# Retention stage: outputs of both chunks of a pair together, scores of both chunks together at the end of TensorE's step, their masks in the next step

## What is computed

```python
# X (1, 2048, 128); L, D, F, H = 4, 128, 256, 8; DH = 16
def _retention(x, Wq, Wk, Wv, Wg, Wo, gn_s, gn_b, Dm, cos, sin):
    Q = (x @ Wq).reshape(B, S, H, DH)
    K = (x @ Wk).reshape(B, S, H, DH)
    V = (x @ Wv).reshape(B, S, H, DH)
    Q = _rotate(Q, cos, sin)
    K = _rotate(K, cos, -sin)
    att = jnp.einsum('bnhd,bmhd->bhnm', Q, K) * Dm     # Dm: causal decay per head
    Y = jnp.einsum('bhnm,bmhd->bnhd', att, V)
    ...                                                 # Y normalised per head, * gn_s + gn_b
    G = jax.nn.swish(x @ Wg)
    return G * Y @ Wo
for i in range(L):
    Yr = _retention(_layer_norm(X, ln_scale, ln_bias), Wq[i], ...) + X
    X = jax.nn.gelu(_layer_norm(Yr, ln_scale, ln_bias) @ W1[i]) @ W2[i] + Yr
```

## Time and profile before

| what | value |
|---|---|
| time, median of 3 runs | 599.06 us (598.79 to 599.08) |
| the profiled execution, its own time | 599.84 us |
| its span in the profile | 598.0 us |
| PE busy | 539.7 us, 90% of the span |
| DVE busy | 492.8 us, 82% |
| ACT busy | 359.2 us, 60% |
| POOL busy | 210.1 us, 35% |
| granted PE clock, mean | 0.984 |

### The profile page before, as it was taken

How to read it: one execution, slowest core, us unless ns; L and a number is a source line. 1 busy time by engine, 2 the same in 40 slices (tenths; PEclk the granted TensorE clock), 3 DMA queues, 4 the chain that set the end, 5 groups by cost and what they waited for, 6 DMA issues and landing times. The chain is left out here.

```text
span 598.0 us, 14018 instructions
## 1 busy us (share of the span) xinstructions
PE 539.7 (90%) x4372; PEld 413.8 (69%) x4372; DVE 492.8 (82%) x1825; ACT 359.2 (60%) x830; POOL 210.1 (35%) x223
## 2 busy tenths in 40 slices
PE   0899999999999999999988897898299999897994
PEld 0666787878878788787866465896155777466992
DVE  6799888988888888888899797788958999993663
ACT  2677887777877778777767675686234220132760
POOL 2354353442533425335250055375200000072671
PEclk9999999999999999999999999899699999998999
DMA  8949999993000000000000311222100000012315
GB/s 304 372 141 189 180 184 179 186 188 58 3 1 2 2 2 3 2 1 2 2 2 2 103 43 55 80 78 76 32 0 1 2 0 2 1 50 58 101 54 158
DMA packets 61130, 43.29 MB, mean 72 GB/s; under 512 B 4641, under 2 KB 58273, under 8 KB 60801
## 3 DMA queue, kind: packets, MB, share of 16 engines
q1 hardware_dynamic: 56160, 35.42, 28.7%
q0 software_dynamic: 2496, 5.13, 2.6%
q10 hardware_dynamic: 2400, 1.84, 1.0%
HBM read 18.38 MB, written 24.01 MB: 71 GB/s over the span
## 5 line engine op out<-in xcount | busy, mean ns | idle before, releaser
L471 POOL TENSOR_TENSOR att<-att,small 128x512 f32<-128x512 f32 x63 | 80.7, 1282 | 170.7 <-ACT att L360 170.7
L368 ACT ACTIVATE xz<-resid,nmr,rs 128x128 f32<-128x128 f32 x128 | 56.7, 503 | 8.6 <-DVE nmr L838 8.6
L1042 POOL DMA_INDIRECT rows_back<-ffn_yt,ffn_front x46 | 47.0, 1021 | 41.5 <-DVE ffn_yt L1393 40.3
L360 ACT ACTIVATE att<-banks 128x512 f32<-128x512 f32 x63 | 38.3, 607 | 38.3 <-PE banks L518 38.3
L1222 PE MATMUL banks<-ffn_xtT,ffn_wt 128*128 128x128 f32 x368 | 51.7, 286 | 2.2 <-DVE ffn_hr L1387 2.2
L709 DVE TENSOR_TENSOR att<-banks,small 128x512 f32<-128x512 f32 x64 | 44.0, 688 | 9.3 <-PE banks L518 9.1
L1222 PEld LDWEIGHTS banks<-ffn_xtT,ffn_wt 128*128 128x128 f32 x368 | 47.4, 202 | 3.1 <-ACT ffn_wt L1069 2.4
L518 PE MATMUL banks<-qexp,qkT 32*128 32x256 f32 x512 | 45.7, 426 | 1.7 <-DVE att L709 1.2
L489 POOL TENSOR_TENSOR qk<-cosq,sinq 128x512 f32<-128x512 f32 x32 | 40.9, 1277 | 13.9 <-DVE cosq L765 13.5
L894 PE MATMUL banks<-small 128*128 128x512 f32 (+1 forms) x74 | 31.4, 543 | 13.6 <-POOL osc_taps L1465 11.5
L1033 POOL DMA_INDIRECT rows_in<-ffn_front,ffn_slot x32 | 31.9, 998 | 29.0 <-DVE ffn_slot L1305 20.5
(11 more groups left out here) (259 smaller groups left out, 1443.8 us busy)
## 6 DMA issues: line engine op xcount, KB each, us to landing
rows_in<-zero_rows SPq DMA_DIRECT2D x16, 1032.0 KB, 18.3
shared_tab<-in_rot SPq DMA_DIRECT2D x3, 1024.0 KB, 12.6
routed_sb<-in_routed SPq DMA_DIRECT2D x1, 3072.0 KB, 12.3
ffn_front<-rows_in SPq DMA_DIRECT2D x46, 64.5 KB, 1.9
ffn_yg<-rows_back SPq DMA_DIRECT2D x8, 256.0 KB, 3.7
shared_tab<-in_rot ACTq DMA_DIRECT2D x1, 1024.0 KB, 10.3
w<-in_W SPq DMA_DIRECT2D x2, 512.0 KB, 7.3
times<-in_times SPq DMA_DIRECT2D x1, 1024.0 KB, 4.9
```

Source lines behind the costliest of these rows:

```text
L360: act.activation(att[:, c, HALF:HEADS].rearrange("p (r e) n -> p r e n", e=PER_TILE), b_att[:, 2:4, c], ACT.Copy).then_inc(s["att_raw"], 1)
L368: ins = act.activation(xz[:, n], resid[:, (g % GROUPS) * 2 + n % 2], ACT.Identity, scale=rs[:, n:n + 1], bias=nmr[:, n:n + 1])
L471: pool.tensor_tensor(att[:, c, HALF:HEADS], att[:, c, HALF:HEADS], spread(causal.unsqueeze(1), 1, HALF), ALU.mult) \
L1042: pool.indirect_dma_start(rows_back, bass.IndirectOffsetOnAxis(ap=token, axis=0), yt[:, j % RING], None).then_inc(stored[j % RING], 16)
```

## The change

The scores of both chunks of group t-1 stand together at the end of PE's step t, as eight matmuls behind one wait, and raise `att_ready` once. Their copies and masks, for both chunks, stand in the next step on ACT, POOL and DVE. Both chunks' outputs stand together: first the two matmuls with the state (each raises the new semaphore `state_read`, for which the next state waits in place of `y_ready`), then the sixteen with the masked scores. The turn of the outputs and its copy (`outputs_turned` on PE, `outputs_kept` on ACT) move into the step after. All four programs are cut into named functions, and put in a new order, with an order of their own for the last steps.

ACT and POOL:

```diff
                 def raw_scores(g, c):
 
                     wait(act, s["y_ready"], 2 * g + c - 1)
-                    wait(act, s["att_ready"], 2 * g + c + 1)
+                    wait(act, s["att_ready"], g + 1)
                     act.activation(att[:, c, HALF:HEADS].rearrange("p (r e) n -> p r e n", e=PER_TILE),
                                    b_att[:, 2:4, c], ACT.Copy).then_inc(s["att_raw"], 1)
...
-                    if coming(t):
-                        for n in range(2):
-                            c = 2 * (t + AHEAD_IN) + n
-                            ins = act.activation(resid[:, c], xin[:, c], ACT.Identity, scale=rs[:, 4 + n:5 + n],
-                                                 bias=nmr[:, 4 + n:5 + n])
...
                     lo, hi = (0 if on(0) else 2), (4 if on(6) else 2)
                     if hi > lo:
                         wait(act, s["xzt_ready"], t + 1)
                         act.activation(xzT[:, lo:hi].rearrange("p a b -> p (a b)"),
                                        b_xv[:, lo * P:hi * P], ACT.Identity,
                                        scale=lnsb[:, 0:1], bias=lnsb[:, 1:2]).then_inc(s["xzT_sb"], 1)
-                    if on(1):
...
-                        wait(act, s["gyt_ready"], g - 3)
-                        wait(act, s["ytok_ready"], g + 1)
-                        act.activation(yc[:, v].rearrange("p a b -> p (a b)"), b_y[:, 0:256], ACT.Copy) \
-                           .then_inc(s["yc_sb"], 1)
+                        g, v = t - 1, (u - 1) % RING
+                        wait(act, s["qkT_sb"], g + 1)
+                        wait(act, s["att_ready"], g - 1)
+                        for e in range(PER_TILE):
+                            ins = act.activation(qexp[:, v % 2, :, e, :], qkT[:, v, 0], ACT.Copy,
+                                                 scale=headmask[:, e:e + 1])
+                        ins.then_inc(s["qexp_act"], 1)
+
+                def step(t, u, on):
+                    if t < STEPS + 2:
+                        tables_doubled(t, u, on)
+                        mlp_rows(t, u, on)
+                        rows(t, u, on)
+                        input_rows(t, u, on)
+                        values_copied(t, u, on)
+                        first_raw(t, u, on)
+                        outputs_kept(t, u, on)
+                        second_raw(t, u, on)
+                        heads_scaled(t, u, on)
+                        squares(t, u, on)
+                        qk_copied(t, u, on)
+                        rows_copied(t, u, on)
+                        outputs_copied(t, u, on)
+                        mlp_hidden(t, u, on)
+                        queries_by_head(t, u, on)
...
-                def step(t, u, on):
+                def constants(t, u, on):
...
+                def rotated(t, u, on):
                     if on(1):
                         g, v = t - 1, (u - 1) % RING
                         wait(pool, s["rot_ready"], g + 1)
...
+                def first_masked(t, u, on):
+                    if on(2):
+                        masked(t - 2, 0)
+
+                def second_masked(t, u, on):
                     if on(2) and t != STEPS + 1:
                         masked(t - 2, 1)
-                    if on(1):
-                        masked(t - 1, 0)
+
+                def step(t, u, on):
+                    constants(t, u, on)
+                    rotated(t, u, on)
+                    first_masked(t, u, on)
+                    second_masked(t, u, on)
```

PE:

```diff
-                def scores(g, v, c):
-
+                def scores(g, v):
                     wait(pe, s["qexp_act"], g + 1)
-                    wait(pe, s["att_raw"], 2 * g + c)
-                    wait(pe, s["att_masked"], 2 * g + c)
-                    for r in range(4):
-                        rows = slice(32 * r, 32 * r + 32)
-                        ins = pe.matmul(b_att[:, r, c], qkT[rows, v, 1, c],
-                                        qexp[rows, v % 2, c], start=True, stop=True)
+                    wait(pe, s["att_raw"], 2 * g)
+                    wait(pe, s["att_masked"], 2 * g)
+                    for c in range(2):
+                        for r in range(4):
+                            rows = slice(32 * r, 32 * r + 32)
+                            ins = pe.matmul(b_att[:, r, c], qkT[rows, v, 1, c],
+                                            qexp[rows, v % 2, c], start=True, stop=True)
                     ins.then_inc(s["att_ready"], 1)
 
-                def outputs(g, v, c):
-
-                    wait(pe, s["state_ready"], 2 * g + c)
-                    if c == 0:
-                        wait(pe, s["yc_sb"], g)
-                    wait(pe, s["att_masked_rest"], 2 * g + c + 1)
-                    wait(pe, s["att_masked"], 2 * g + c + 1)
-                    out = b_y[:, c * P:c * P + P]
-                    pe.matmul(out, state[:, c], qkT[:, v, 0, c], start=True, stop=False,
-                              skip_group_check=True)
-                    for e in range(2):
-                        for q in range(4):
-                            ins = pe.matmul(out[32 * q:32 * q + 32, :],
-                                            ve[:, v, c, q, e].rearrange("p j d -> p (j d)"),
-                                            att[:, c, 2 * q + e, :], start=False, stop=(e == 1),
-                                            skip_group_check=True)
-                    ins.then_inc(s["y_ready"], 1)
+                def outputs(g, v):
+                    wait(pe, s["yc_sb"], g)
+                    wait(pe, s["state_ready"], 2 * g + 1)
+                    for c in range(2):
+                        pe.matmul(b_y[:, c * P:c * P + P], state[:, c], qkT[:, v, 0, c], start=(c == 0), stop=False,
+                                  skip_group_check=True).then_inc(s["state_read"], 1)
+                    for c in range(2):
+                        wait(pe, s["att_masked_rest"], 2 * g + c + 1)
+                        wait(pe, s["att_masked"], 2 * g + c + 1)
+                        for e in range(2):
+                            for q in range(4):
+                                ins = pe.matmul(b_y[32 * q:32 * q + 32, c * P:c * P + P],
+                                                ve[:, v, c, q, e].rearrange("p j d -> p (j d)"),
+                                                att[:, c, 2 * q + e, :], start=False, stop=(e == 1),
+                                                skip_group_check=True)
+                        ins.then_inc(s["y_ready"], 1)
...
+                def outputs_turned(t, u, on):
+                    if on(3):
+                        wait(pe, s["yT_sb"], t - 2)
+                        for c in range(2):
+                            ins = pe.transpose(b_y[:, c * P:c * P + P], yT[:, c], eye)
+                        ins.then_inc(s["ytok_ready"], 1)
...
+                def both_scores(t, u, on):
+                    if on(1):
+                        scores(t - 1, (u - 1) % RING)
+
+                def step(t, u, on):
+                    if t == 4:
+                        pe.wait_ge(s["loaded_w"], 16 * N_W)
+                    if t < STEPS + 2:
+                        outputs_turned(t, u, on)
+                        project(t, u, on)
+                        mlp_down(t, u, on)
+                        heads_turned(t, u, on)
+                        rows_turned(t, u, on)
+                        qk_turned(t, u, on)
+                        keys_by_values(t, u, on)
+                        both_outputs(t, u, on)
+                        mlp_up(t, u, on)
+                        queries_keys(t, u, on)
+                        values_gate(t, u, on)
+                        both_scores(t, u, on)
+                    else:
+                        project(t, u, on)
+                        outputs_turned(t, u, on)
+                        mlp_down(t, u, on)
+                        heads_turned(t, u, on)
+                        rows_turned(t, u, on)
+                        mlp_up(t, u, on)
```

DVE (the bodies of the named functions are those of before, unless shown):

```diff
-                    wait(dve, s["att_ready"], 2 * g + c + 1)
+                    wait(dve, s["att_ready"], g + 1)
                     dve.tensor_tensor(att[:, c, 0:HALF].rearrange("p (r e) n -> p r e n", e=PER_TILE),
...
-                    wait(dve, s["y_ready"], 2 * g + c)
+                    wait(dve, s["state_read"], 2 * g + c)
                     dve.scalar_tensor_tensor(out=state[:, 1 - c], in0=state[:, c],
...
+                def step(t, u, on):
+                    if t < STEPS + 2:
+                        row_statistics(t, u, on)
+                        head_variances(t, u, on)
+                        aggregated(t, u, on)
+                        first_keys_values(t, u, on)
+                        newton = chain_begun(t, on)
+                        next(newton)
+                        next(newton)
+                        next(newton)
+                        next(newton)
+                        second_state(t, u, on)
```

(19 more changed lines are left out.)

241 lines of the change are left out of this document (150 added, 91 removed).

## The result

The changed kernel takes 591.48 us in the median (590.44 to 594.09, four runs) against 599.07 for the kernel before on the same chip: a ratio of 0.9875, 95% interval 0.9841 to 0.9909. It is faster, by 7.6 us where 8.1 were predicted, and inside the range predicted. The profiled execution took 590.93 us, with a span of 589.1 us (before: 598.0).

A forecast was written before the change was run, and what follows sets the result against it. PE was taken as the bound: step 9.32 - 0.75 + 0.28 = 8.85 us; 24 x 0.47 = 11.3, plus 1.1 at the start, less 4.3 at the end, gains 8.1: median 591.0 us, range 586.5 to 595.5 (chance 0.76).

The forecast's parts named there:

- PE's list, 0.75 us less: PE, full steps: merging score bursts saves 0.42, output bursts 0.29, leaving scores into transposes 0.04; list 9.32 to 8.57 us.
- the 0.04 for leaving the scores into transposes: PE, each step: scores left once into transposes (0.06 open) instead of twice into matmuls (0.10), saving 0.04 us.
- The rival that each pass pays its load: PE's merged scores: passes 3 and 4 take 0.32 us each, 6.8 us less gain, 597.8 us; chance 0.07.
- The three waits, 0.28 us: PE, each step: round trips losing cover add 0.15 (GELU), 0.09 (MLP added) and 0.04 us (scaled heads); step 8.85.
- the rival without waits: PE, full steps: the three waits don't appear, step 8.57 us, 6.7 us more gain, 584.3 us; chance 0.06.
- The masks: ACT and POOL: copies and products end about 3.7 us after the scores, PE needs them at 4.2; 0.5 us slack.
- The slower rival: Masks decide if ACT's first raw copy comes 1.5 us after the scores: step 9.4 us, 604.2 us; chance 0.06.
- The start, a gain of 1.1: Up to 75.3 us, pipeline filling: laid out, the new order gains 1.1 us, at most 3.3, perhaps nothing.
- The end, a loss of 4.3: Last steps: 3.3 us from step 33's exposed chain, MLP addition 0.7 later, last five steps lose 0.4; given as 4.3.
- the low end: Step 33: smaller estimate of its loss, 2.4 us, from 12.2 against 9.82 us before; 3.3 was taken.
- The MLP of step 32 is added 0.7 later: End of the pipeline: the MLP addition stands 0.7 us later in its step, part of the end's loss.
- the last five steps: End of the pipeline: these steps lose 0.4 us, part of the end's loss.

The follow-up runs named there:

- The splits: Changed kernel with outputs chunk by chunk again, back to back (605.35 us, ratio 1.0073), or with scores parted by the turn of the outputs (603.68 us, 1.0047).
- turn_before_gate: Changed kernel with the turn of the outputs moved between queries/keys and values/gate: ratio 0.9852, step 8.73 us.
- tail_raw_first: Changed kernel where, in step 33 alone, ACT copies the first raw scores ahead of the MLP's rows: step 33 took 12.96 us.
- turn_tail_fill: Changed kernel with turn before the gate, raw copy first in step 33, and short constant matmuls in PE's idle places at the end: 588.34 us, ratio 0.9827.
- best_again: Repeat of turn_tail_fill, without further edits: ratio 0.9803, step 8.73 us.
- mask_behind_early: best_again with DVE's first mask put behind the projection's addition and the gate in steps 5 and 6: step 8.73 us, no median given.

## Why the prediction was right

**PE's list, 0.75 us less: right.** The splits give 0.34 for the outputs (0.29 predicted) and 0.41 for the scores (0.42). They were measured inside the new order, so each also holds what a split hides or uncovers of a wait, and they can't part the 0.04 for leaving the scores into transposes; the sum, 0.74, agrees with 0.75.

**The rival that each pass pays its load: refuted.** Passes 2 and 3 of the burst cost 0.22 each, 0.44 for both, not 0.64.

**The three waits, 0.28 us: right.** Read from spacings they are 0.15, 0.08 and 0.02, where 0.15, 0.09 and 0.04 were predicted (L677's first record starts 0.136 behind L667's last instead of 0.109, and 0.164 ahead of its second instead of 0.109; L690's first stands 0.130 ahead of its second instead of 0.111); turn_before_gate took the first away and gave 0.10 net. Thus the rival without waits is refuted too, and the step is 8.83 (8.85 predicted). Over 24 steps the gain is 12.05 us instead of 11.3; the mean step is 8.82.

**The masks: right.** 0.5 us of slack predicted, 0.5 read. The slower rival's condition, a first raw copy 1.5 us behind the scores, did not come up: it starts 0.60 behind (0.54 predicted). Its price was added wrongly: 0.5 and another 0.5 on top of 8.85 make 9.85, not 9.4.

**The start, a gain of 1.1: wrong.** It became a loss of 0.5 in the first profile, and lies between 0.3 less and 1.7 more than before in all kernels of the new order. The step that failed is "laid out, the new order gains 1.1 there", which took PE's list for the limit wherever PE was mostly busy. In these steps DVE's list is, as shown above, and the change takes nothing from DVE. What the clock did in the first two steps blurs the size. Behind them, from the third rotation to the eighth, four profiles of the new order agree on a loss of 0.38 us (43.36 against 42.98). What the change adds there stays open.

**The end, a loss of 4.3: a third too large.** The timelines of step 33 in the change:

```profile
290.63 0.42 DVE L849 TENSOR_TENSOR resid<-banks,resid 128x256 f32<-128x256 f32 x1
...
296.29 1.15 PE L583 MATMUL banks<-qexp,qkT 32*128 32x256 f32 x16 [1.54 <-ACT qexp L481]
...
299.60 0.68 PE L622 MATMUL banks<-wo,gyT 128*128 128x128 f32 x4 [1.79 <-DVE gyT L929]
...
301.89 0.69 DVE L816 TENSOR_TENSOR att<-banks,small 128x512 f32<-128x512 f32 x1 [1.50 <-POOL att L524]
...
302.82 0.42 DVE L849 TENSOR_TENSOR resid<-banks,resid 128x256 f32<-128x256 f32 x1
```

The chain is the one that was laid out, and its length is right, 302.82 - 290.63 = 12.19 us (12.2 predicted): PE waits 1.54 for the queries by head, DVE 1.50 for POOL before the mask of the rest. Against before's 9.82 that is 2.4, which was the low end; I took 3.3, by setting before's step at 8.9 because "some instructions there run slower than elsewhere". But a time that the measured kernel spent is spent, whatever slowed it: the difference has to be made against its row. Half of that 0.9 can be named from the DVE timeline of the kernel before:

```profile
307.89 0.65 DVE L178 SCALAR_TENSOR_TENSOR vt<-vt 128x22 f32<-128x22 f32 x1
```

It lasts 0.65 us instead of 0.18, beside a product of POOL's (L471) that runs from 307.22 to 308.49: the same stall as in tail_raw_first, already there before the change, and gone in the change, where POOL's product begins only at 300.59. The MLP of step 32 is added 0.7 later, as predicted, and the last five steps gave 0.3 where 0.4 of loss was predicted. Together 2.8. (The prediction's own terms, 3.3, 0.7 and 0.4, add up to 4.4, not 4.3.)

So the total, 8.9 us by the spans and 7.6 by the medians against 8.1, owes something to luck. Two errors nearly cancel, 1.6 at the start and 1.5 at the end, and the full steps gave 0.75 more than the 11.3 predicted. The forecast also took over from the kernel before that the median lies 0.8 under the profiled execution; in the change it lies 0.55 above it. These 1.3 us turn 0.8 more than predicted, by the profiles, into 0.5 less, by the medians.

## What to carry to other kernels

Read what a burst in another tile shape costs beside its streaming (here 0.3 to 0.4 us each) before merging or splitting one, and then add every round trip that loses the work in front of it: here 0.25 of 0.75 us went back, and the order alone was a loss. Ask in every stretch for itself which engine never idles: the same edit gave 0.5 us a step where PE was full and nothing where DVE was. Before giving POOL or DVE a two-operand product at a new time, look what small chain link of the other engine it will stand beside; a record of the unchanged kernel that is longer than its like (here L178, 0.65 for 0.18) shows such a stall before anything is changed.

## What the hardware showed that I had not expected

**A DVE instruction can wait for the whole rest of a POOL product.** L178 has two operands in SBUF and 22 elements. In the four profiles where it starts beside POOL's mask (tail_raw_first, turn_tail_fill, best_again, mask_behind_early) it lasts 1.24 us, which is what is left of the mask, 1.20, and 0.04 more; where it doesn't, 0.18. L971 went from 0.42 to 1.49 when the mask was moved beside it. Not every DVE instruction is hit. The masks of the scores, which read one operand from PSUM, started beside a POOL product 811 times in the fourteen profiles, and none was longer than 0.69 us, against a median of 0.68. Two operands in SBUF aren't needed, though: L1015 of the change, a TENSOR_SCALAR on 22 elements with one, lasts 0.23 to 0.52 us beside POOL's products in its first steps, for 0.17 otherwise. The other way round the price was small: POOL's sum of the rotation halves started 377 times beside DVE's scaling of the outputs (L956 in the change, two operands in SBUF, 0.25 us of it left), and lasted 1.39 us instead of 1.27. The Trainium skill (SBUF — State Buffer, SBUF: two separate sides) calls it an exclusive lock on a shared pair of ports. The runs agree where POOL was first; where DVE was first, POOL's record grew by 0.12, less than what DVE had left. That the lock makes a link of 22 elements cost seven times its length on a critical chain is what I had not reckoned with.

**The granted clock after a wait isn't the same in every execution.** In the change the window 286 to 328 us has 1.00 in one profile and 0.92 in another, with the same waits of 1.54 and 1.79 us on PE in it; in tail_raw_first it fell within the wait of 2.86 us. And the unchanged rest of the span took 260.2 to 263.4 us in most profiles, but 266.6 and 265.6 in two; in that of turn_before_gate the granted clock was 0.71 from 330 to 365 us, where the change had 1.00. That is the size of most differences in these experiments, so the beat and the chains in the profile decided them, not the medians.
